# Two more rounding steps in each direction when the hidden activations are quantized

## The chip, the cores and the metric

The kernel runs on all eight cores of one Trainium2 chip. Each core computes one of eight batch rows with the same program and its own input, and the cores exchange nothing. The metric is the device time in microseconds of the slowest core. Each core has a TensorE (matrix products, called PE in the profile), a VectorE (DVE), a ScalarE (ACT), a GpSimd (POOL) and a SyncE (SP); the last two mostly issue DMA transfers here.

## The reference

One transformer layer on x of 8 x 2048 x 1024: causal attention with 16 heads and rotary embedding, a residual with layer norm, then a gated feed-forward block in which activations and weights are quantized, and again a residual with layer norm.

```python
def _act_quant(x):
    scale = 127.0 / jnp.clip(jnp.max(jnp.abs(x), axis=-1, keepdims=True), 1e-05)
    xq = jnp.clip(jnp.round(x * scale), -128.0, 127.0) / scale
    return x + jax.lax.stop_gradient(xq - x)

def _bitlinear(x, w):
    return jnp.einsum('bsi,oi->bso', _act_quant(x), _weight_quant(w))

x = _layernorm(x + _L0_attn_ref(x, L0_attn_w_qkv, L0_attn_w_out), axis=-1)
gate = jax.nn.silu(_bitlinear(x, w_gate))      # 1024 -> 4096
up = _bitlinear(x, w_up)                       # 1024 -> 4096
y = _bitlinear(gate * up, w_down)              # 4096 -> 1024
x = _layernorm(x + y, axis=-1)
```

`_weight_quant` makes every weight -1, 0 or 1 times one scale. What matters here is `_act_quant` of `gate * up`: each of 2048 rows has 4096 values that are scaled to at most 127 and rounded to an integer.

## The kernel before, in words

The first part of the program, up to about 1600 us of the span, computes attention, the first layer norm, the quantized input of the feed-forward block and the three weight matrices of -1, 0 and 1, which it leaves in device memory. The change does not touch it.

The second part is the feed-forward block. The 2048 rows are cut into four super-tiles (`j` from 0 to 3) of four row tiles (`k` from 0 to 3) with 128 rows each. For a super-tile TensorE runs the gate and up matmuls (lines 1653 and 1667), 32 groups of 128 x 512. ScalarE applies silu (line 1451), VectorE multiplies the two (line 1394) and keeps the largest absolute value of each row (lines 1400 to 1408). The product stays in SBUF as `h_h`, 4096 values a row.

Then the row tile is quantized by VectorE in `qchunks`, in four chunks of 1024 columns. A chunk is six instructions: scale and shift by 512 into `h_z` (line 1301), convert to int16 in `h_i` (1305), two compares that find out how the conversion rounded (1307 and 1310, into `h_u2` and `h_u3`), an add of the two results (1313), and the sum with an offset into `h_hq` (1316). TensorE turns `h_hq` by transposes into the PSUM tiles `p6t` (line 1688), and VectorE copies them to `h_hqT` (line 1373, written by `evacs`), eight copies a row tile.

The down projection (line 1627) of a super-tile is run by TensorE after the gate and up matmuls of the next super-tile, in two halves of 512 columns with 16 steps each. GpSimd loads its weights `h_td` (line 1581) into two buffers, one step at a time, each as soon as TensorE has emptied a buffer. At the end of a half VectorE copies four PSUM tiles to `h_os` with a scale (line 1329, written by `osbatch`). The second layer norm follows (`chainA`, `chainB`).

VectorE's order is written out by hand, and an engine runs its instructions in that order. For a super-tile after the first it is:

```python
qchunks(j, 0)
if j >= 1:
    osbatch(j - 1, 0)
qchunks(j, 1)
evacs(j, 0, 8)
qchunks(j, 2)
evacs(j, 8, 16)
qchunks(j, 3)
if j >= 1:
    osbatch(j - 1, 1)
evacs(j, 16, 24)
```

The other two `chainA` calls, the last copies and `chainB` come behind it, and then the scales and products of the next super-tile. Every instruction of `qchunks` has a drain before it, so that the one before has written its result. On TensorE the order is: gate and up of `j`, down of `j - 1`, the transposes of `j`, gate and up of `j + 1`.

Of the kernel before, what the change touches and what calls it, by code (L numbers as in the profile page):

```python
# [12 lines left out]
ALU = mybir.AluOpType  # L13
# [53 lines left out]
def build_program(stop_phase=99, debug=(), max_pairs=None, dbg_mode=None):  # L67
# [32 lines left out]
    with es:  # L100
# [5 lines left out]
        def CC(v):  # L106
            return s_consts[:, CIDX[v]:CIDX[v] + 1]
# [55 lines left out]
        def mk(stack, name, shape, dt=F32, side=None):  # L163
            kw = {} if side is None else {"side": side}
            return stack.enter_context(nc.sbuf_tensor(name, shape, dt, **kw))
# [1029 lines left out]
        s_z2 = mk(scH, "h_z2", [128, 1024])  # L1195
        s_i2 = mk(scH, "h_i2", [128, 1024], I16)
        s_u2 = mk(scH, "h_u2", [128, 1024], BF16)
        s_u3 = mk(scH, "h_u3", [128, 1024], BF16)
# [26 lines left out]
        def sc2c(j, k, w):  # L1225
            i = (j % 2) * NTS * 5 + k * 5 + SC2W[w]
            return s_sc2[:, i:i + 1]

        def hqb(j, k):
            return s_hq[(j * NTS + k) % 2]  # L1230
# [35 lines left out]
        def V(key, fn, waits=(), drain=False):  # L1266
            ve_ops.append((key, fn, waits, drain))
# [24 lines left out]
        def qchunks(j, k):  # L1292
            gt = j * NTS + k
            for c in range(4):
                cols = slice(c * 1024, (c + 1) * 1024)
                w = []
                if c == 0 and gt >= 2:
                    pj, pk = divmod(gt - 2, NTS)
                    w.append(("te", ("tr", pj, pk, 7)))
                V(("z2", j, k, c), lambda v, j=j, k=k, c=c, cols=cols:  # L1300
                    v.tensor_scalar(s_z2[:], s_h[k][:, cols],
                                    sc2c(j, k, "zq"), CC(512.0),
                                    ALU.mult, ALU.add),
                    waits=w, drain=True)
                V(None, lambda v: v.tensor_copy(s_i2[:], s_z2[:]),
                    drain=True)
                V(None, lambda v: v.scalar_tensor_tensor(  # L1307
                    s_u2[:], s_z2[:], -0.5, s_i2[:], ALU.add, ALU.is_ge),
                    drain=True)
                V(None, lambda v: v.scalar_tensor_tensor(  # L1310
                    s_u3[:], s_z2[:], 0.5, s_i2[:], ALU.add, ALU.is_ge),
                    drain=True)
                V(None, lambda v: v.tensor_tensor(
                    s_u2[:], s_u2[:], s_u3[:], ALU.add), drain=True)
                V(("hq", j, k, c), lambda v, j=j, k=k, c=c, cols=cols:
                    v.scalar_tensor_tensor(hqb(j, k)[:, cols], s_i2[:],
                                           -513.0, s_u2[:], ALU.add,
                                           ALU.add), drain=True)

        def osbatch(jd, h2):  # L1320
# [56 lines left out]
        for j in range(NSUP):  # L1377
# [14 lines left out]
            for gi in range(32):  # L1392
# [18 lines left out]
                if o == NCH - 1:  # L1411
                    qhead(j, k)
# [9 lines that stand above are left out]
# [19 lines left out]
        for j in range(NSUP):  # L1441
            for gi in range(32):
# [6 lines left out]
                elif j >= 1:  # L1449
# [4 lines left out]
                    drain=(gi <= 1))  # L1454
# [319 lines left out]
```

How the kernel before makes its waits and increments, by code:

```python
        @block.sync  # L202
        def _(sy):
            sy.wait_ge(dS.h, ph0_sync)
            for c in range(4):
                if c >= 1:
                    sy.wait_ge(tbv.h, c * 26)
                dS.dinc(sy.dma_start(out=s_gm[:],
                                     in_=d_t128[:, c * 512:(c + 1) * 512]))
                dS_tch[c] = dS.n
# [4 lines left out]
        @block.vector  # L215
        def _(v):
            for c in range(4):
                sl = slice(c * 512, (c + 1) * 512)
                v.wait_ge(dS.h, dS_tch[c])
                v.drain()
                tbv.inc(v.tensor_scalar(s_ga[:], s_gm[:],
                                        s_ifr[:, 0:1], CC(0.0),
# [36 lines left out]
                                            CC(0.0), ALU.mult, ALU.add))  # L259
                    v.drain()
                    tbv.inc(v.tensor_tensor(s_gs[:], s_gs[:], s_gm[:],
                                            ALU.subtract))
                    v.drain()
                    tbv.inc(v.tensor_scalar(s_gs[:], s_gs[:], CC(PI_CL),
                                            CC(NPI_CL), ALU.min, ALU.max))
                    v.drain()
                    if br == 0:
                        tb_sin[c] = tbv.n
                        v.wait_ge(tbs.h, 2 * c + 1)
                        v.drain()
                        tbv.inc(v.tensor_scalar(s_sin[:, sl], s_sin[:, sl],
                                                s_ifr[:, 2:3], CC(0.0),
# [1447 lines left out]
    @block.sync  # L1720
# [1 line left out]
        for c in ctrs:  # L1722
            if c.n:
                sy.wait_ge(c.h, c.n)
```

## Time and profile before

| | us |
|---|---|
| median of the timed runs (3) | 2928.35 |
| lowest and highest run | 2926.47, 2933.09 |
| profiled execution, device time | 2930.23 |
| its span on the slowest core (core 6) | 2928.6 |
| spans of the eight cores | 2906.9 to 2928.6 |
| VectorE busy, share of the span | 1355.8, 46% |
| TensorE busy, share of the span | 1604.0, 55% |

The profile is of one execution, on the slowest core unless another is named. Engine times are microseconds from the start of the span. A row of a group gives the line of the kernel, the engine, the operation, what is written from what, the shape, the count, the busy time and the mean of one, then the idle time before and what ended it. In an order of time, the first number is the start and the second the duration; in brackets stands the idle time before and what ended it.

### The profile page before, as it was taken

How to read it: one execution, taken by the hardware profiler on the slowest of the kernel's cores; microseconds unless marked ns; L12 is line 12 of the kernel's file. 1: busy time of each engine (PE TensorE's matmuls, PEld its weight loads, DVE VectorE, ACT ScalarE, POOL GpSimd, SP SyncE). 2: the span in 40 equal slices, each digit the busy share in tenths (PEclk: the TensorE clock that was granted, in tenths of full speed). 3: DMA queues.
4: the chain of work that ended last, by engine and by line, in shares of the span. 5: the costliest groups of instructions: out<-in, count | busy, mean ns of one | idle time of the engine just before them, and what ended most of it. 6: DMA issues, size and time to landing. Idle time of an engine off the chain costs nothing.

```text
span 2928.6 us, 23780 instructions; the slowest of 8 cores (2906.9 to 2928.6 us)
## 1 busy us (share of the span) xinstructions
PE 1604.0 (55%) x6348; PEld 649.7 (22%) x6348; DVE 1355.8 (46%) x2151; ACT 751.8 (26%) x1186; POOL 430.0 (15%) x684
## 2 busy tenths in 40 slices
PE   0597059999996731111110590496529762796263
PEld 0243013323332210000000240242214321342121
DVE  4404433343344343333343148745584649455733
ACT  0230036665664034443444120020012100210010
POOL 1000211111111123333334000001100020002021
PEclk9799558888887565555555795799859995899687
DMA  9000223333332179999999632044213420332032
GB/s 155 11 1 15 72 72 99 100 96 98 100 111 76 34 153 198 207 201 203 210 239 232 168 116 72 29 144 129 65 47 122 141 94 22 115 101 83 25 115 101
DMA packets 166725, 320.12 MB, mean 109 GB/s; under 512 B 30003, under 2 KB 99894, under 8 KB 166582
## 3 DMA queue, kind: packets, MB, share of 16 engines
q0 software_dynamic: 71168, 216.31, 31.1%
q1 hardware_dynamic: 95430, 102.29, 11.3%
q8 instruction: 58, 0.95, 0.1%
q14 instruction: 69, 0.57, 0.1%
HBM read 249.08 MB, written 71.30 MB: 109 GB/s over the span
## 4 chain that ended last, share of the span: by engine, by line
PE 42%; DMA 25%; DVE 16%; issue 7%; ACT 6%; DVEq 3%; POOL 2%; ACTq 0%; SPq 0%; POOLq 0%
DMA h_td<-ternd 7%; PE p6a L1653 7%; PE p6a L1667 7%; PE p_sc L537 6%; PE p_av L554 6%; PE p6a L1627 5%; DMA t_wst<-wuT 5%; DMA t_wst<-wgT 5%; PE p_qk L316 4%; DMA t_wst<-wdT 3%; PE p_sc L544 3%; ACT a_E L565 2%; PE p_qk L330 2%; PE p_R L797 2%; DVE h_u L1307 2%
## 5 line engine op out<-in xcount | busy, mean ns | idle before, releaser
L565 ACT ACTIVATE a_E<-p_sc 128x512 bf16<-128x512 f32 x640 | 333.5, 627 | 190.3 <-PE p_sc L544 102.7
L1627 PE MATMUL p6a<-h_td,h_hqT 128*128 128x512 bf16 x1024 | 268.7, 413 | 154.0 <-DMA h_td<-ternd 142.5
L537 PE MATMUL p_sc<-a_q,a_k 64*128 64x512 bf16 x640 | 241.9, 418 | 148.9 <-DMA e_sel<-sel 119.3
L1653 PE MATMUL p6a<-h_tg,h_xql 128*128 128x512 bf16 x1024 | 250.4, 389 | 88.8 <-DMA h_tu<-ternu 47.2
L999 PE MATMUL p_tr<-c_ident,f_xqtm 128*128 128x128 bf16 x128 | 16.2, 307 | 442.4 <-DVE f_xqtm L1090 442.4
L1667 PE MATMUL p6a<-h_tu,h_xql 128*128 128x512 bf16 x1024 | 244.5, 382 | 0.0
L1581 POOL DMA_DIRECT2D h_td<-ternd x128 | 92.0, 719 | 956.9 <-PE p6a L1627 935.2
L1451 ACT ACTIVATE h_sg<-p6a,h_sc 128x512 bf16<-128x512 f32 x128 | 88.0, 687 | 460.8 <-PE p6a L1653 316.0
L1688 PE MATMUL p6t<-c_ident,h_hq 128*128 128x128 bf16 x512 | 51.6, 280 | 281.2 <-DVE h_hqT L1373 250.1
L578 DVE TENSOR_REDUCE t_msum<-t_wst 128x1 f32<-128x1024 f32 x96 | 116.1, 1219 | 189.7 <-DMA t_wst<-wdT 69.3
L1394 DVE TENSOR_TENSOR h_h<-h_sg,p6a 128x512 f32<-128x512 bf16 x128 | 87.8, 686 | 247.9 <-PE p6a L1667 242.4
L554 PE MATMUL p_av<-a_E,a_v 128*65 128x512 bf16 x640 | 183.2, 439 | 2.9 <-ACT a_E L565 2.9
L1115 ACT ACTIVATE t_ta<-t_wst,p_thr 128x1024 bf16<-128x1024 f32 x96 | 109.9, 1145 | 276.7 <-DMA t_wst<-wuT 108.3
L316 PE MATMUL p_qk<-a_xfm,a_wqk 128*128 128x512 bf16 x512 | 116.1, 391 | 106.2 <-DMA a_wv<-wqkv 74.7
L1457 ACT ACTIVATE h_sg<-h_os 128x512 bf16<-128x512 f32 x16 | 10.1, 630 | 632.6 <-DVE h_os L1338 632.6
L1627 PEld LDWEIGHTS p6a<-h_td,h_hqT 128*128 128x128 bf16 x1024 | 99.8, 104 | 321.8 <-issue 243.4
L1653 PEld LDWEIGHTS p6a<-h_tg,h_xql 128*128 128x128 bf16 x1024 | 101.6, 100 | 214.3 <-issue 98.5
L1667 PEld LDWEIGHTS p6a<-h_tu,h_xql 128*128 128x128 bf16 x1024 | 101.2, 99 | 124.3 <-issue 6.2
L537 PEld LDWEIGHTS p_sc<-a_q,a_k 64*128 64x128 bf16 x640 | 56.9, 95 | 321.1 <-issue 309.7
L1044 DVE TENSOR_SCALAR f_st<-f_st,c_consts 128x1 f32<-128x1 f32 x16 | 4.4, 273 | 266.4 <-ACT f_tr L1126 266.4
L544 PE MATMUL p_sc<-a_masks,c_ident 128*128 128x512 bf16 x256 | 119.7, 468 | 0.0
L999 PEld LDWEIGHTS p_tr<-c_ident,f_xqtm 128*128 128x128 bf16 x128 | 12.4, 138 | 449.4 <-issue 449.4
(155 smaller groups left out, 2246.4 us busy)
## 6 DMA issues: line engine op xcount, KB each, us to landing
t_wst<-wgT POOLq DMA_DIRECT2D x64, 512.0 KB, 7.0
t_wst<-wuT POOLq DMA_DIRECT2D x64, 512.0 KB, 6.1
t_wst<-wdT POOLq DMA_DIRECT2D x64, 512.0 KB, 5.9
h_td<-ternd POOLq DMA_DIRECT2D x128, 256.0 KB, 3.2
h_tg<-terng SPq DMA_DIRECT2D x32, 1024.0 KB, 7.6
h_tu<-ternu SPq DMA_DIRECT2D x32, 1024.0 KB, 10.0
f_xt<-x SPq DMA_DIRECT2D x16, 512.0 KB, 9.3
y1s<-f_y1n SPq DMA_DIRECT2D x16, 512.0 KB, 6.3
```

The source lines that it names most:

```text
L316: mm = t.matmul(pb[:], s_wqk[:, kc * 2048 + sl * 128: kc * 2048 + (sl + 1) * 128], s_xfm[:, kc * S + ntile * 512: kc * S + (ntile + 1) * 512],
L537: mm = t.matmul(pb[:], s_k[hp * 64: hp * 64 + 64, ch * S + kc * 128: ch * S + (kc + 1) * 128], s_q[hp * 64: hp * 64 + 64, ch * S + j * 512 ...
L544: mm = t.matmul(pb[:], s_ident[:], s_masks[:, r * 512:(r + 1) * 512], start=False, stop=True)
L554: mm = t.matmul(pv[:], s_v[:, vbase: vbase + 65], s_E[:, kc * 512:(kc + 1) * 512], start=(kc == 0), stop=(kc == nkc[(h, j)] - 1))
L565: se.inc(s.activation(s_E[:, kc * 512:(kc + 1) * 512], p_sc[kc % 4][:], AF.Exp, bias=-CSTAB, scale=0.125))
L578: tpA.inc(v.tensor_reduce(s_msum[:, i6:i6 + 1], s_wst[i6 % 3][:], AXX, ALU.add, apply_absolute_value=True))
L1115: ts2.inc(s.activation(s_ta[i6 % 4][:], s_wst[(NWCH + i6) % 3][:], AF.Sign, bias=s_thr[:, 4 + mi6:5 + mi6], scale=1.0))
L1451: SEO(("silu", j, gi), lambda s, j=j, gi=gi, k=k: s.activation(s_sg[gi % 2][:], p_a[0 if gi % 2 == 0 else 2][:], AF.Silu, scale=sc2c(j, k, ...
L1581: dTd[dn % 2].dinc(g.dma_start(out=outap, in_=inap))
L1627: mm = t.matmul(p_a[k][:], s_hqT[k][:, kc * 128:(kc + 1) * 128], s_td[dn % 2][:, kk * 512:(kk + 1) * 512], start=(g2 == 0 and kk == 0), st ...
L1653: mm = t.matmul(pg[:], s_xql[j % 2][:, kc * 512 + k * 128:kc * 512 + (k + 1) * 128], s_tg[gs % 2][:, kc * 512:(kc + 1) * 512], start=(kc = ...
L1667: mm = t.matmul(pu[:], s_xql[j % 2][:, kc * 512 + k * 128:kc * 512 + (k + 1) * 128], s_tu[gs % 2][:, kc * 512:(kc + 1) * 512], start=(kc = ...
```

## The change

Where `qchunks` compared with two offsets (-0.5 and 0.5) and added the two results, it now compares with four (-0.5, -1.5, 0.5 and 1.5) and adds each to the running sum. The constant that is added at the end goes from -513 to -514, so that the quantized value is the same wherever the two further compares give 1 and 0.

```diff
                 V(None, lambda v: v.scalar_tensor_tensor(
                     s_u2[:], s_z2[:], -0.5, s_i2[:], ALU.add, ALU.is_ge),
                     drain=True)
-                V(None, lambda v: v.scalar_tensor_tensor(
-                    s_u3[:], s_z2[:], 0.5, s_i2[:], ALU.add, ALU.is_ge),
-                    drain=True)
-                V(None, lambda v: v.tensor_tensor(
-                    s_u2[:], s_u2[:], s_u3[:], ALU.add), drain=True)
+                for off in (-1.5, 0.5, 1.5):
+                    V(None, lambda v, off=off: v.scalar_tensor_tensor(
+                        s_u3[:], s_z2[:], off, s_i2[:], ALU.add, ALU.is_ge),
+                        drain=True)
+                    V(None, lambda v: v.tensor_tensor(
+                        s_u2[:], s_u2[:], s_u3[:], ALU.add), drain=True)
                 V(("hq", j, k, c), lambda v, j=j, k=k, c=c, cols=cols:
                     v.scalar_tensor_tensor(hqb(j, k)[:, cols], s_i2[:],
-                                           -513.0, s_u2[:], ALU.add,
+                                           -514.0, s_u2[:], ALU.add,
                                            ALU.add), drain=True)
```

Behind the compares, the lines of the changed kernel are one higher than before. The order of VectorE at the end of row tile 0 of super-tile 1, before: the last chunk, and then the first of the four copies behind the first half of the down projection, which waits for TensorE (`te`).

```order
L1301 TENSOR_SCALAR h_z2<-h_h0,h_sc2,c_consts 128x1024
L1305 CAST h_i2<-h_z2 128x1024
L1307 SCALAR_TENSOR_TENSOR h_u2<-h_z2,h_i2 128x1024
L1310 SCALAR_TENSOR_TENSOR h_u3<-h_z2,h_i2 128x1024
L1313 TENSOR_TENSOR h_u2<-h_u2,h_u3 128x1024
L1316 SCALAR_TENSOR_TENSOR h_hq0<-h_i2,h_u2 128x1024
L1329 TENSOR_SCALAR h_os0<-p6a0,h_sc2,c_consts 128x512 [waits te]
L1329 TENSOR_SCALAR h_os1<-p6a1,h_sc2,c_consts 128x512
```

After:

```order
L1301 TENSOR_SCALAR h_z2<-h_h0,h_sc2,c_consts 128x1024
L1305 CAST h_i2<-h_z2 128x1024
L1307 SCALAR_TENSOR_TENSOR h_u2<-h_z2,h_i2 128x1024
L1311 SCALAR_TENSOR_TENSOR h_u3<-h_z2,h_i2 128x1024
L1314 TENSOR_TENSOR h_u2<-h_u2,h_u3 128x1024
L1311 SCALAR_TENSOR_TENSOR h_u3<-h_z2,h_i2 128x1024
L1314 TENSOR_TENSOR h_u2<-h_u2,h_u3 128x1024
L1311 SCALAR_TENSOR_TENSOR h_u3<-h_z2,h_i2 128x1024
L1314 TENSOR_TENSOR h_u2<-h_u2,h_u3 128x1024
L1317 SCALAR_TENSOR_TENSOR h_hq0<-h_i2,h_u2 128x1024
L1330 TENSOR_SCALAR h_os0<-p6a0,h_sc2,c_consts 128x512 [waits te]
L1330 TENSOR_SCALAR h_os1<-p6a1,h_sc2,c_consts 128x512
```

The chunk has ten instructions in the place of six, and what stands behind it is the same. The order of VectorE between row tiles 2 and 3 of super-tile 1, before: row tile 2's last chunk, the eight copies of row tile 1's transposes, and the first instruction of row tile 3.

```order
L1301 TENSOR_SCALAR h_z<-h_h,h_sc,c_consts 128x1024
L1305 CAST h_i<-h_z 128x1024
L1307 SCALAR_TENSOR_TENSOR h_u<-h_z,h_i 128x1024
L1310 SCALAR_TENSOR_TENSOR h_u<-h_z,h_i 128x1024
L1313 TENSOR_TENSOR h_u<-h_u 128x1024
L1316 SCALAR_TENSOR_TENSOR h_hq<-h_i,h_u 128x1024
L1373 COPY h_hqT<-p6t 128x512 [waits te] x8
L1301 TENSOR_SCALAR h_z<-h_h,h_sc,c_consts 128x1024 [waits te]
```

After:

```order
L1301 TENSOR_SCALAR h_z<-h_h,h_sc,c_consts 128x1024
L1305 CAST h_i<-h_z 128x1024
L1307 SCALAR_TENSOR_TENSOR h_u<-h_z,h_i 128x1024
L1311 SCALAR_TENSOR_TENSOR h_u<-h_z,h_i 128x1024
L1314 TENSOR_TENSOR h_u<-h_u 128x1024
L1311 SCALAR_TENSOR_TENSOR h_u<-h_z,h_i 128x1024
L1314 TENSOR_TENSOR h_u<-h_u 128x1024
L1311 SCALAR_TENSOR_TENSOR h_u<-h_z,h_i 128x1024
L1314 TENSOR_TENSOR h_u<-h_u 128x1024
L1317 SCALAR_TENSOR_TENSOR h_hq<-h_i,h_u 128x1024
L1374 COPY h_hqT<-p6t 128x512 [waits te] x8
L1301 TENSOR_SCALAR h_z<-h_h,h_sc,c_consts 128x1024 [waits te]
```

Here too the four further instructions stand ahead of the copies, in each of the four chunks of row tile 2. No instruction of another engine has moved.

## Rows read from the trace of the kernel before

**Rows 1.** The page: the span, and busy time of each engine.

```profile
span 2928.6 us, 23780 instructions; the slowest of 8 cores (2906.9 to 2928.6 us)
...
PE 1604.0 (55%) x6348; PEld 649.7 (22%) x6348; DVE 1355.8 (46%) x2151; ACT 751.8 (26%) x1186; POOL 430.0 (15%) x684
```

**Rows 2.** Stretches: us, busy of PE, PEld, DVE, ACT, POOL (count), granted clock, DMA share, GB/s.

```profile
1758.00:1877.00 119.00, 13.69 (x130) 12.33 (x128) 108.43 (x142) 0.00 (x0) 0.00 (x0) 0.54 0.15 44
...
2101.00:2202.00 101.00, 21.80 (x162) 14.75 (x160) 84.68 (x148) 9.83 (x23) 2.49 (x4) 0.60 0.10 37
...
2412.00:2512.00 100.00, 21.07 (x156) 14.22 (x153) 84.67 (x148) 9.57 (x23) 2.48 (x4) 0.60 0.10 38
...
2720.00:2793.00 73.00, 12.46 (x125) 10.84 (x123) 67.63 (x92) 2.89 (x8) 2.49 (x4) 0.59 0.06 22
```

**Rows 3.** Waits of TensorE after 1600 us: total, times, longest.

```profile
PE p6t L1688 <- DVE h_hqT L1373: 250.1, 12, 27.9
...
PE p6t L1688 <- DVE h_hq L1316: 31.1, 1, 31.1
```

**Rows 4.** Groups of VectorE after 1600 us, the compare and the add.

```profile
L1310 DVE SCALAR_TENSOR_TENSOR h_u<-h_z,h_i 128x1024 bf16<-128x1024 f32 x64 | 78.4, 1225 | 5.9
...
L1313 DVE TENSOR_TENSOR h_u<-h_u 128x1024 bf16<-128x1024 bf16 x64 | 44.3, 692 | 5.9
```

**Rows 5.** VectorE in order of time, two chunks of super-tile 0.

```profile
1763.74 0.81 DVE L1301 TENSOR_SCALAR h_z<-h_h,h_sc,c_consts 128x1024 f32<-128x1024 f32 x1
...
1770.17 0.81 DVE L1301 TENSOR_SCALAR h_z<-h_h,h_sc,c_consts 128x1024 f32<-128x1024 f32 x1
```

**Rows 6.** VectorE in order of time, super-tiles 1 to 3: the long waits.

```profile
2046.20 2.97 DVE L1329 TENSOR_SCALAR h_os<-p6a,h_sc,c_consts 128x512 f32<-128x512 f32 x4 [27.38 <-PE p6a L1627]
...
2101.80 2.74 DVE L1373 COPY h_hqT<-p6t 128x512 bf16<-128x512 bf16 x8 [26.92 <-PE p6t L1688]
...
2361.97 2.96 DVE L1329 TENSOR_SCALAR h_os<-p6a,h_sc,c_consts 128x512 f32<-128x512 f32 x4 [23.19 <-PE p6a L1627]
...
2412.08 2.74 DVE L1373 COPY h_hqT<-p6t 128x512 bf16<-128x512 bf16 x8 [21.42 <-PE p6t L1688]
...
2670.42 2.97 DVE L1329 TENSOR_SCALAR h_os<-p6a,h_sc,c_consts 128x512 f32<-128x512 f32 x4 [20.88 <-PE p6a L1627]
...
2720.11 2.74 DVE L1373 COPY h_hqT<-p6t 128x512 bf16<-128x512 bf16 x8 [21.00 <-PE p6t L1688]
```

**Rows 7.** The same on core 0, super-tile 3.

```profile
2648.44 2.96 DVE L1329 TENSOR_SCALAR h_os<-p6a,h_sc,c_consts 128x512 f32<-128x512 f32 x4 [15.83 <-PE p6a L1627]
...
2696.75 2.74 DVE L1373 COPY h_hqT<-p6t 128x512 bf16<-128x512 bf16 x8 [19.59 <-PE p6t L1688]
```

**Rows 8.** TensorE in order of time after pauses, and once it runs.

```profile
1645.24 3.57 PE L1653 MATMUL p6a<-h_tg,h_xql 128*128 128x512 bf16 x8 [47.24 <-DMA h_tu<-ternu]
...
2130.73 3.57 PE L1688 MATMUL p6t<-c_ident,h_hq 128*128 128x128 bf16 x32 [25.66 <-DVE h_hqT L1373]
...
2202.16 3.57 PE L1653 MATMUL p6a<-h_tg,h_xql 128*128 128x512 bf16 x8 [20.94 <-ACT h_sg L1451]
...
2207.87 1.89 PE L1653 MATMUL p6a<-h_tg,h_xql 128*128 128x512 bf16 x8
```

**Rows 9.** Loads at line 1581: us, POOL busy (count), granted clock, DMA share, GB/s.

```profile
2364.90:2390.60 25.70, 5.70 (x8) 0.93 0.25 79
2673.40:2699.00 25.60, 5.74 (x8) 0.93 0.26 80
2390.60:2411.90 21.30, 4.26 (x6) 1.00 0.40 124
2699.00:2720.00 21.00, 4.26 (x6) 1.00 0.40 130
```

**Rows 10.** Groups of TensorE after 1600 us, the down projection.

```profile
L1627 PE MATMUL p6a<-h_td,h_hqT 128*128 128x512 bf16 x1024 | 268.7, 413 | 154.0 <-DMA h_td<-ternd 142.5 <-DVE h_os L1329 5.0 <-DVE h_h L1394 4.0
```

## The prediction

> **What bounds the kernel now.** Start with the totals [rows 1]: TensorE is busy 55% of the span and VectorE 46%, so neither is full and an average decides nothing. The question is which engine ends last in the stretch that the edit touches. The edit lies in the quantization of the hidden activations, which only runs after about 1760 us of the span, so the second view is the busy time by stretch [rows 2]. The reader sees four stretches, one for each super-tile, in which VectorE is busy for 108.43 of 119, 84.68 of 101, 84.67 of 100 and 67.63 of 73 us, while TensorE does 12 to 22 us of work. There VectorE sets the pace, and TensorE waits for it.
>
> The third view, TensorE's waits by tile, says the same from the other side [rows 3]: 250.1 us in 12 waits for the copies of the transposed activations (`h_hqT`), and 31.1 us in one wait for the first quantized tile. These are waits for VectorE's queue, in which the quantization of the next tile stands ahead of the copies.
>
> The fourth view is VectorE's own order of time. In super-tile 0, chunk follows chunk without a gap: one starts at 1763.74, the next at 1770.17 [rows 5], 6.43 us each. In super-tiles 1 to 3 VectorE does idle at two places, and there alone beside this work [rows 6]. After row tile 0 it waits for the first half of the down projection (27.38, 23.19 and 20.88 us), and after row tile 1 for the second half and the transposes behind it (26.92, 21.42 and 21.00 us). After row tiles 2 and 3 no such row exists.
>
> **The change, part by part.** It removes nothing. In each chunk it adds two compares of the kind of line 1310 and two adds of the kind of line 1313, with the same shapes, types and buffers, each behind a drain. The immediate values (-1.5, 1.5, and -514 for -513) change no shape. No DMA, wait or step of another engine is added or moved.
>
> Price of a chunk, from the groups by line [rows 4]: a compare takes 1225 ns, an add 692 ns. The gap before each is 5.9 us over 64, 0.092 us. So 2 x 1.225 + 2 x 0.692 + 4 x 0.092 = 4.20 us on top of 6.43. A row tile has 4 chunks: 16.81 us more (25.7 becomes 42.5). There are 16 row tiles: 268.9 us of VectorE work in all.
>
> Which of the 16 lie on the path:
> - Super-tile 0, four tiles: VectorE has no idle time, and the transposes and then the gate and up matmuls of super-tile 1 stand behind it. All four count: 67.2 us.
> - Super-tiles 1 to 3, row tile 0: the work grows into the wait for the down projection's first half. The waits of 20.88 to 27.38 us exceed 16.81, so 4 to 10.6 us are left and nothing shows. If that cover were gone, 16.8 us would show each time.
> - Row tile 1: the same with the second half, 21.00 to 26.92 us, so 4.2 to 10.1 us are left. Nothing shows.
> - Row tiles 2 and 3: VectorE runs without a wait from the first copies to the start of the next super-tile. Two tiles in three super-tiles: 6 x 16.81 = 100.9 us show.
>
> Sum: 10 x 16.81 = 168.1 us show and 6 x 16.81 = 100.9 us are hidden. What is late next after the hidden ones is still the down projection.
>
> The cover must hold on every core, since the slowest counts. The shortest wait of all cores is core 0's in super-tile 3, 15.83 us, with 19.59 us after it [rows 7]: there 1.0 us would show. I cost it at nothing.
>
> Two costs the trace of before shows only indirectly. First, TensorE's clock: the pauses that show grow from about 26 us (25.66 in one) to 42 us. In the four stretches the granted clock is already 0.54 to 0.60 [rows 2], near the lower of the two levels (1.2 of 2.4 GHz), and the first eight matmuls take 3.57 us after a pause of 20.94 us as after one of 47.24 us, against 1.89 us later on; the pause of 25.66 us ends in transposes [rows 8]. A longer pause costs what the short one does, and no new pause is made. I take 0; the ends are 0 and 13 x 1.7 = 22 us, if each of the 13 waits of [rows 3] paid once more what a restart costs (3.57 - 1.89).
>
> Second, GpSimd's loads of the down weights (`h_td`), which run beside the covered tiles. GpSimd issued 8 loads in 25.70 us and 8 in 25.60 us while VectorE quantized, and 6 in 21.30 and 6 in 21.00 us while it was idle [rows 9]: 3.2 us a load in the first case, 3.5 in the second. A busy VectorE does not slow them, so I take 0 here too.
>
> The Trainium skill ("SBUF — State Buffer", "Summary: rules for kernel authors") speaks against that: it says that descriptor generation for a DMA from GpSimd's queue starves while VectorE is in one of its faster modes. An add of 692 ns for as many elements as a compare of 1225 ns looks like such a mode. The same page, under "Who interferes with whom", says that an operation on two tensors has no mode that takes both ports, and the rows side with that. By the first rule the time would be that of the second rival below.
>
> The profiled execution took 2930.23 us (span 2928.6 us and 1.6 around it), 1.9 above the median of the timed runs, 2928.35. So 2930.2 + 168.1 = 3098.3 for a profile, and 3096.5 for the median: I forecast 3097 us, 5.7% slower.
>
> **The rivals.**
> 1. No cover: the six tiles beside the down projection show as well. For it: only 4 us of slack is left in super-tile 3 of the profiled core. Against it: the waits of rows 6 end with TensorE and not with VectorE, and they are longer than 16.81 us in all six cases there. It would give 2928.4 + 268.9 = 3197 us; one uncovered tile gives 16.8 us of that.
> 2. Starved loads: each load that falls into the 16.8 us of added work in a half of the down projection is held up by one added instruction, at most 1.225 us. With one load in 3.2 us that is 5 loads, 6.4 us in each of six halves: 39 us, so 3135 us. For it: TensorE waits 142.5 us for these loads already [rows 10], so a delay shows. Against it: rows 9.
> 3. Row tile 3's share hides behind the next super-tile's matmuls, which TensorE begins before VectorE is done. For it: two groups do run ahead. Against it: then TensorE stops for 20.94 us [rows 8], for the activation that needs VectorE's scales. In super-tiles 1 and 2 this would take back 2 x 16.8 us: 3063 us.
> 4. Not slower: the down projection's loads run ahead while VectorE holds the rest up, so that this stage goes at full rate. Its 1024 matmuls take 268.7 us and wait 142.5 us [rows 10]; at 1.89 us for eight they would take 242 us. That gives back 169 us against 168.1, and the time stays at 2928 us. It decides only if the whole of the waits goes and the clock stays up throughout. Against it: a load is issued only when TensorE has emptied one of two buffers, so it cannot run ahead during a pause, and a shorter half would uncover row tiles 0 and 1.
>
> That the change doesn't do what it says is excluded by the order of instructions, where VectorE has 64 x 4 more.
>
> **How the numbers follow.** Forecast 86%, rival 1 (in whole or for two or more tiles) 4%, rival 2 5%, rival 3 3%, rival 4 2%. Within the forecast, the spread of the runs before (2926.47 to 2933.09 us), single uncovered tiles on one core and part of the 22 us for the clock move the time by -12 to +20 us: 3085 to 3117. Towards rival 2 and rival 3 I widen it to 3080 to 3122, which leaves out most of the rivals' 14%. What a measurement can tell from no change is about 0.2%, 6 us; only rival 4 comes near it: faster 0.01, same 0.01, slower 0.98.
>
> **What would show it.** VectorE's busy time should rise by 64 x 3.83 = 245 us, with 192 compares at line 1311 of 1225 ns and 192 adds at line 1314 of 692 ns (128 more of each). A chunk should take 10.63 us. The six waits after row tiles 0 and 1 should shrink to 4 to 11 us, and TensorE's waits for `h_hqT` should grow by about 151 us, nine times 16.8, since the first of super-tile 0 is counted as a wait for `h_hq` (31.1 to 47.9 us). The gate, up and down stretches should keep their length. I am wrong if a wait of rows 6 vanishes and TensorE then waits in the down projection for VectorE, if loads of `h_td` take longer than 3.2 us each beside the compares, or if the compares with another constant take another time.

## The result and the profile after

The changed kernel takes 3099.28 us (median of 8 runs, 3089.37 to 3105.26) against 2931.02 us for the kernel before (8 runs, 2924.19 to 2938.24). The ratio is 1.0571, with a 95% interval from 1.0553 to 1.059: 168.3 us slower by the medians, 162 to 173 us by the interval. The forecast was 3097 us and 168.1 us more; that the two differ by 0.2 us is luck, since the interval is 11 us wide. Some executions are in a slower state, in which the cores of a die show a lower granted clock; the ratios here and below leave them out and the medians of the experiments do not, so a ratio need not be the quotient of two medians.

The page of the profiled execution after, whose slowest core is now core 4:

```profile
span 3103.6 us, 24181 instructions; the slowest of 8 cores (3071.5 to 3103.6 us)
...
PE 1578.4 (51%) x6237; PEld 647.0 (21%) x6348; DVE 1601.7 (52%) x2407; ACT 751.5 (24%) x1186; POOL 429.0 (14%) x684
```

VectorE's busy time rose from 1355.8 [rows 1] to 1601.7 us, by 245.9, on 256 more instructions. The span grew by only 175 us of these 246 (the medians differ by 168). TensorE's share fell from 55% to 51%, since the same program of TensorE stands in a longer span.

The stretches in which VectorE sets the pace, cut at the same events as in [rows 2], with the same columns:

```profile
1765.80:1952.30 186.50, 13.60 (x129) 12.21 (x128) 169.68 (x205) 0.00 (x0) 0.00 (x0) 0.52 0.10 28
2174.30:2309.50 135.20, 20.96 (x160) 15.20 (x159) 115.56 (x180) 9.84 (x23) 2.49 (x4) 0.56 0.07 27
2520.90:2654.20 133.30, 19.74 (x155) 14.00 (x153) 115.36 (x180) 9.58 (x23) 2.48 (x4) 0.56 0.08 28
2862.30:2969.20 106.90, 12.37 (x124) 10.80 (x122) 98.26 (x124) 2.89 (x8) 2.48 (x4) 0.55 0.05 15
```

They last 186.5, 135.2, 133.3 and 106.9 us in the place of 119, 101, 100 and 73: 67.5, 34.2, 33.3 and 33.9 us more, 168.9 together. That is the loss of the medians; the other 6 us of the 175 lie outside and are no more than executions of one kernel differ by. VectorE's busy time in the four grew by 61.3, 30.9, 30.7 and 30.6 us, and the gaps before the added instructions make up most of the rest, while TensorE's stayed at 12 to 21 us.

TensorE's waits by tile after 1600 us:

```profile
PE p6t L1689 <- DVE h_hqT L1374: 401.8, 12, 44.7
...
PE p6t L1689 <- DVE h_hq L1317: 47.9, 1, 47.9
...
PE p6a L1628 <- DVE h_os L1330: 6.8, 12, 1.5
```

The wait for the copies grew from 250.1 [rows 3] to 401.8 us, by 151.7 in the same 12 waits, and the one for the first quantized tile from 31.1 to 47.9 us.

The compares and adds of VectorE, by line:

```profile
L1311 DVE SCALAR_TENSOR_TENSOR h_u<-h_z,h_i 128x1024 bf16<-128x1024 f32 x192 | 235.2, 1225 | 17.7
L1314 DVE TENSOR_TENSOR h_u<-h_u 128x1024 bf16<-128x1024 bf16 x192 | 132.9, 692 | 17.7
```

There are 192 of each in the place of 64 [rows 4], at the same 1225 and 692 ns, with 17.7 us of gaps over 192, 0.092 us each. That is two compares and two adds more in each of 64 chunks; the two compares are one in each direction, and not two in each as the title can be read.

Two chunks of super-tile 0 in VectorE's order of time (start, then duration):

```profile
1771.51 0.81 DVE L1301 TENSOR_SCALAR h_z<-h_h,h_sc,c_consts 128x1024 f32<-128x1024 f32 x1
...
1782.15 0.81 DVE L1301 TENSOR_SCALAR h_z<-h_h,h_sc,c_consts 128x1024 f32<-128x1024 f32 x1
```

A chunk takes 10.64 us, where it took 6.43 [rows 5].

The six places after row tiles 0 and 1 of super-tiles 1 to 3, in VectorE's order of time (core 4):

```profile
2122.56 2.96 DVE L1330 TENSOR_SCALAR h_os<-p6a,h_sc,c_consts 128x512 f32<-128x512 f32 x4 [11.63 <-PE p6a L1628]
...
2175.13 2.94 DVE L1374 COPY h_hqT<-p6t 128x512 bf16<-128x512 bf16 x8 [7.09 <-PE p6t L1689]
...
2470.39 2.96 DVE L1330 TENSOR_SCALAR h_os<-p6a,h_sc,c_consts 128x512 f32<-128x512 f32 x4 [8.15 <-PE p6a L1628]
...
2521.01 2.74 DVE L1374 COPY h_hqT<-p6t 128x512 bf16<-128x512 bf16 x8 [5.07 <-PE p6t L1689]
...
2807.33 2.96 DVE L1330 TENSOR_SCALAR h_os<-p6a,h_sc,c_consts 128x512 f32<-128x512 f32 x4
...
2862.39 2.74 DVE L1374 COPY h_hqT<-p6t 128x512 bf16<-128x512 bf16 x8 [9.51 <-PE p6t L1689]
```

The waits that were 21 to 27 us [rows 6] are 11.63, 7.09, 8.15, 5.07, none and 9.51 us. At the fifth, in super-tile 3, the cover is used up. That was not this core alone: on cores 3 to 7 no wait of 1 us is left there, on cores 0 to 2 it is 1.9 to 4.9 us. In the kernel before this place was the tightest, with 15.83 us on core 0 [rows 7] and 16.4 to 20.9 us on the other seven, and the 20.88 us of the profiled core 6 [rows 6] was the longest of the eight. It cost little: TensorE's waits for the copies of line 1330 are 6.8 us in all on core 4, and 5.0 to 8.6 us over the eight cores, where they were 4.3 to 8.1 us before.

### The profile page after: what moved, and what is told of

Same layout as the page of the kernel before. It is cut to its first block, busy times and chain, and to the rows that moved or that the text cites. A ratio compares the mean times of both kernels' runs of the same rounds, so it can differ in the third digit from the quotient of the medians.

```text
span 3103.6 us, 24181 instructions; the slowest of 8 cores (3071.5 to 3103.6 us)
## 1 busy us (share of the span) xinstructions
PE 1578.4 (51%) x6237; PEld 647.0 (21%) x6348; DVE 1601.7 (52%) x2407; ACT 751.5 (24%) x1186; POOL 429.0 (14%) x684
## 4 chain that ended last, share of the span: by engine, by line
PE 37%; DMA 23%; DVE 21%; issue 7%; ACT 6%; DVEq 3%; POOL 2%; ACTq 0%; SPq 0%; POOLq 0%
PE p6a L1654 6%; PE p6a L1668 6%; DMA h_td<-ternd 6%; PE p_av L554 5%; DVE h_u L1311 5%; DMA t_wst<-wuT 5%; PE p_sc L537 5%; DMA t_wst<-wgT 5%; PE p6a L1628 4%; DMA t_wst<-wdT 4%; PE p_qk L316 3%; DVE h_u L1314 3%; ACT a_E L565 3%; PE p_sc L544 3%; PE p_qk L330 2%
## 5 line engine op out<-in xcount | busy, mean ns | idle before, releaser
L1628 PE MATMUL p6a<-h_td,h_hqT 128*128 128x512 bf16 x1003 | 263.0, 407 | 160.0 <-DMA h_td<-ternd 144.9
L1689 PE MATMUL p6t<-c_ident,h_hq 128*128 128x128 bf16 x512 | 52.2, 283 | 449.8 <-DVE h_hqT L1374 401.8
L1311 DVE SCALAR_TENSOR_TENSOR h_u<-h_z,h_i 128x1024 bf16<-128x1024 f32 x192 | 235.2, 1225 | 17.7
L1314 DVE TENSOR_TENSOR h_u<-h_u 128x1024 bf16<-128x1024 bf16 x192 | 132.9, 692 | 17.7
L1689 PEld LDWEIGHTS p6t<-c_ident,h_hq 128*128 128x128 bf16 x512 | 46.6, 131 | 456.2 <-issue 453.6
```

Source lines behind the costliest of these rows:

```text
L1311: V(None, lambda v, off=off: v.scalar_tensor_tensor(s_u3[:], s_z2[:], off, s_i2[:], ALU.add, ALU.is_ge), drain=True)
L1314: V(None, lambda v: v.tensor_tensor(s_u2[:], s_u2[:], s_u3[:], ALU.add), drain=True)
L1628: mm = t.matmul(p_a[k][:], s_hqT[k][:, kc * 128:(kc + 1) * 128], s_td[dn % 2][:, kk * 512:(kk + 1) * 512], start=(g2 == 0 and kk == 0), st ...
L1689: mm = t.transpose(pb[:, kk * 128:(kk + 1) * 128], hqb(j, k)[:, kc * 128:(kc + 1) * 128], s_ident[:])
```

## The experiments

In these experiments "covered" means row tiles 0 and 1 of super-tiles 1 to 3, and "exposed" the other ten. The edits of the first four are shown against the changed kernel, those of the last two against the kernel before. All times are compared with the kernel before, run again beside them. In the second to the fourth the loop over `offs` and the constant `base` stand as in the first and are left out here.

### The change in the covered row tiles alone

```diff
+                offs = (-1.5, 0.5, 1.5) if j >= 1 and k < 2 else (0.5,)
+                base = -514.0 if j >= 1 and k < 2 else -513.0
-                for off in (-1.5, 0.5, 1.5):
+                for off in offs:
...
-                                           -514.0, s_u2[:], ALU.add,
+                                           base, s_u2[:], ALU.add,
```

> The four further instructions of a chunk stand only in row tiles 0 and 1 of super-tiles 1 to 3 (6 of 16 row tiles); the other ten are as in the kernel before. Theory A (the down projection covers these six): the time stays at that of before, 2931 us within 6. Rival U (every row tile costs the same share of the measured 168 us): +63 us, 2994. Rival N (nothing is covered): 6 x 16.8 = +101 us, 3032. Rival S (GpSimd's weight loads are held up beside the added work): up to +39 us, 2970, and a longer down projection in the trace. In the trace, by A, VectorE's two waits of each super-tile shrink from 21 to 27 us to 4 to 11 us.

Measured: 2921.76 us against 2925.69, ratio 1.0011 (0.998 to 1.0041): no difference, at most 12 us more by the upper end. Rivals U (1.022), N (1.035) and the full price of S (1.013) lie outside the interval. VectorE's waits at the six places, core 5:

```profile
2033.52 2.97 DVE L1332 TENSOR_SCALAR h_os<-p6a,h_sc,c_consts 128x512 f32<-128x512 f32 x4 [10.57 <-PE p6a L1630]
...
2082.94 2.74 DVE L1376 COPY h_hqT<-p6t 128x512 bf16<-128x512 bf16 x8 [3.89 <-PE p6t L1691]
...
2341.95 2.96 DVE L1332 TENSOR_SCALAR h_os<-p6a,h_sc,c_consts 128x512 f32<-128x512 f32 x4 [4.26 <-PE p6a L1630]
...
2395.75 2.74 DVE L1376 COPY h_hqT<-p6t 128x512 bf16<-128x512 bf16 x8 [8.30 <-PE p6t L1691]
...
2651.09 2.96 DVE L1332 TENSOR_SCALAR h_os<-p6a,h_sc,c_consts 128x512 f32<-128x512 f32 x4 [1.82 <-PE p6a L1630]
...
2700.11 2.74 DVE L1376 COPY h_hqT<-p6t 128x512 bf16<-128x512 bf16 x8 [3.53 <-PE p6t L1691]
```

They are down to 1.82 to 10.57 us. Their sum on this core is 32.4 us, where the same core had 135.2 in the kernel before, some 103 us more. So VectorE did 101 us more work, and its waits paid for all of it. On six other cores no wait of 1 us is left at the fifth place, and the time does not show that.

### The change in the exposed row tiles alone

```diff
+                offs = (0.5,) if j >= 1 and k < 2 else (-1.5, 0.5, 1.5)
+                base = -513.0 if j >= 1 and k < 2 else -514.0
```

> The other ten row tiles alone have the four further instructions: all four of super-tile 0, and row tiles 2 and 3 of super-tiles 1 to 3. Theory A: the whole of the change's price, 10 x 16.8 = +168 us, 3099. Rival U (same share each): +105 us, 3036. Rival S: 168 less what the covered six then cost, up to 39, so 3060. By A, VectorE's two long waits of super-tiles 1 to 3 keep their 21 to 27 us, and TensorE's waits for the transposed copies grow by 9 x 16.8 = 151 us.

Measured: 3086.86 us against 2925.69, ratio 1.0565 (1.0527 to 1.0604), 154 to 177 us more: the price of the whole change (1.0571). U's 105 us is outside, and so is S's 129. TensorE's waits:

```profile
PE p6t L1691 <- DVE h_hqT L1376: 401.1, 12, 44.7
...
PE p6t L1691 <- DVE h_hq L1319: 47.9, 1, 47.9
```

They grew by 151.0 and 16.8 us, as in the changed kernel. VectorE's waits of super-tiles 1 and 3 in this kernel:

```profile
2104.94 2.97 DVE L1332 TENSOR_SCALAR h_os<-p6a,h_sc,c_consts 128x512 f32<-128x512 f32 x4 [28.57 <-PE p6a L1630]
...
2154.82 2.74 DVE L1376 COPY h_hqT<-p6t 128x512 bf16<-128x512 bf16 x8 [21.20 <-PE p6t L1691]
...
2788.31 2.97 DVE L1332 TENSOR_SCALAR h_os<-p6a,h_sc,c_consts 128x512 f32<-128x512 f32 x4 [18.16 <-PE p6a L1630]
...
2839.19 2.74 DVE L1376 COPY h_hqT<-p6t 128x512 bf16<-128x512 bf16 x8 [22.19 <-PE p6t L1691]
```

They lie within what the eight cores showed at these places in the kernel before (26.6 to 30.2, 19.8 to 26.9, 15.8 to 20.9 and 19.6 to 24.5 us), and so do the two of super-tile 2 (20.11 and 24.27 us): they kept their length. So ten row tiles cost everything and six cost nothing that shows, as the sum had it.

### Twice the addition in the covered row tiles

```diff
+                offs = (-2.5, -1.5, 0.5, 1.5, 2.5) if j >= 1 and k < 2 else (0.5,)
+                base = -515.0 if j >= 1 and k < 2 else -513.0
```

> Row tiles 0 and 1 of super-tiles 1 to 3 get twice the addition: eight further instructions in a chunk (offsets -2.5, -1.5, 0.5, 1.5, 2.5 after the first), 33.6 us a row tile; the other ten are as before. Theory A: the cover ends where VectorE's wait ends, so what shows is 33.6 less each wait of the kernel before, 6.2 + 6.7 + 10.4 + 12.2 + 12.7 + 12.6 = 61 us on the profiled core: 2992 us, 2980 to 3005 over the cores. Rival U: +126 us, 3057. Rival N: +202 us, 3133. If VectorE's work beside the down projection were free altogether: 2931.

Measured: 2997.04 us against 2925.69, ratio 1.0244 (1.0201 to 1.0288), 59 to 84 us more; theory A said 61 from one core's waits. TensorE's order of time on core 4 shows where:

```profile
2053.04 6.53 PE L1630 MATMUL p6a<-h_td,h_hqT 128*128 128x512 bf16 x15 [9.01 <-DVE h_os L1332]
...
2114.87 3.57 PE L1691 MATMUL p6t<-c_ident,h_hq 128*128 128x128 bf16 x32 [8.64 <-DVE h_hqT L1376]
...
2385.53 5.30 PE L1630 MATMUL p6a<-h_td,h_hqT 128*128 128x512 bf16 x10 [13.74 <-DVE h_os L1332]
...
2447.35 3.49 PE L1691 MATMUL p6t<-c_ident,h_hq 128*128 128x128 bf16 x32 [9.04 <-DVE h_hqT L1376]
...
2719.38 6.17 PE L1630 MATMUL p6a<-h_td,h_hqT 128*128 128x512 bf16 x15 [17.15 <-DVE h_os L1332]
...
2781.25 3.57 PE L1691 MATMUL p6t<-c_ident,h_hq 128*128 128x128 bf16 x32 [13.30 <-DVE h_hqT L1376]
```

At each of the six places TensorE now waits for VectorE, for the copies after the first half (9.01, 13.74 and 17.15 us) and after the first transposes (8.64, 9.04 and 13.30 us). The sum is 70.9 us, close to the loss by the ratio (0.0244 x 2925.69 = 71.4, with the interval above). The cover is a stock: what the down projection leaves VectorE idle is free, and what goes beyond it shows in full, as far as this one amount can tell. 33.6 us less 70.9 / 6 = 11.8 makes a stock of 21.8 us a place on this core; in the kernel before the same core waited 22.7 us a place (136.1 in all).

### Another kind of work in the covered row tiles

```diff
+                n1 = (5 if c < 2 else 4) if j >= 1 and k < 2 else 0
+                for _n1 in range(n1):
+                    V(None, lambda v: v.tensor_scalar(
+                        s_z2[:], s_z2[:], CC(1.0), CC(0.0),
+                        ALU.mult, ALU.add), drain=True)
```

The compares, the add and the constant of these row tiles are those of the kernel before.

> Row tiles 0 and 1 of super-tiles 1 to 3 get work of about the same length of another kind: 18 operations on one float32 input a row tile (multiply by 1, add 0, in place, the form of line 1301, 812 ns and a gap of 0.092: 16.3 us a row tile) in the place of compares and adds on two inputs. Theory A: what kind of work VectorE does is no matter, it is covered: 2931 us within 6. Rival S in the form of the Trainium skill (SBUF — State Buffer, Who interferes with whom: an operation with one input in a faster mode takes both ports and keeps GpSimd from writing descriptors): each of 5 loads in the added time of a half is held up by up to 0.81 us, 24 us over six halves, 2955, and the issue of a weight load takes longer than 0.72 us.

Measured: 2919.6 us against 2925.69, ratio 0.9991 (0.9967 to 1.0015): no difference. The added operations of VectorE, core 1:

```profile
L1314 DVE TENSOR_SCALAR h_z<-h_z,c_consts 128x1024 f32<-128x1024 f32 x108 | 88.0, 815 | 10.4
```

GpSimd's issues of the down weights on the same core, all 128 of them:

```profile
L1589 POOL DMA_DIRECT2D h_td<-ternd x128 | 95.2, 744 | 955.2 <-PE p6a L1635 933.3 <-issue 21.9
```

And the same group in the kernel with compares and adds in the covered row tiles, core 5:

```profile
L1584 POOL DMA_DIRECT2D h_td<-ternd x128 | 92.2, 721 | 957.9 <-PE p6a L1630 928.3 <-issue 26.5 <-DVE h_u L1313 2.9
```

The issue takes 744 ns on average here and 721 there. Over the eight cores it is 744 to 754 ns in this kernel, against 719 to 729 with the compares and adds and 716 to 723 in the kernel before. These means mix issues beside different work. The table sorts the single issues of these two kernels and of the kernel before (all cores, 1950 to 2800 us of the span) by what VectorE ran during the issue; those beside both kinds of operation are left out.

| VectorE during the issue | mean on a core, us | longest, us |
|---|---|---|
| nothing | 0.71 to 0.72 | 0.72 |
| only operations on two inputs (compares, adds, the sum with an offset) | 0.71 to 0.72 | 0.73 |
| only operations on one input (scale, conversion, the added ones) | 0.74 to 0.80 | 1.11 |

So operations on one input do hold GpSimd up a little, and operations on two inputs not measurably, which is the way the Trainium skill has it ("SBUF — State Buffer", "Who interferes with whom"). It is little: the longest issue took 0.4 us more than one beside an idle VectorE, half the length of an added operation, and over all 128 issues it is some 25 ns each, 3 us in sum, spread beside loads that come every 3.2 us [rows 9]. S, as it was priced (24 us, a ratio of 1.008), is outside the interval.

### The compares without the adds

```diff
+                for off in (-1.5, 1.5):
+                    V(None, lambda v, off=off: v.scalar_tensor_tensor(
+                        s_u3[:], s_z2[:], off, s_i2[:], ALU.add, ALU.is_ge),
+                        drain=True)
```

> In all 16 row tiles the two further compares alone, without their adds (their results are overwritten by the compare that stood there before). Theory A with the price by group: 2 x (1.225 + 0.092) = 2.63 us a chunk, 10.5 us a row tile, ten of them on the path: +105 us, 3036, and so 63 us of the 168 for the adds. Rival: a price per instruction whatever its kind (half of 168): +84 us, 3015. VectorE's long waits of super-tiles 1 to 3 should shrink by 10.5 us each.

Measured: 3018.48 us against 2917.84, ratio 1.0345 (1.0294 to 1.0396), 86 to 116 us more. The 105 us by group is inside, and the 84 by count is just outside. The trace tells them apart better; TensorE's waits:

```profile
PE p6t L1692 <- DVE h_hqT L1377: 345.9, 12, 38.5
...
PE p6t L1692 <- DVE h_hq L1320: 41.6, 1, 41.6
```

Both grew by 10.6 us a wait, 95.8 over nine and 10.5 for the one. An equal price per instruction would have made it 8.4. VectorE's six long waits on core 4 are 73.2 us in sum, where the same core had 136.1 in the kernel before: 10.5 less each, as expected.

### Two instructions in the place of six

```diff
                     v.tensor_scalar(s_z2[:], s_h[k][:, cols],
-                                    sc2c(j, k, "zq"), CC(512.0),
+                                    sc2c(j, k, "zq"), CC(12582912.0),
                                     ALU.mult, ALU.add),
                     waits=w, drain=True)
...
-                    v.scalar_tensor_tensor(hqb(j, k)[:, cols], s_i2[:],
-                                           -513.0, s_u2[:], ALU.add,
-                                           ALU.add), drain=True)
+                    v.tensor_scalar(hqb(j, k)[:, cols], s_z2[:],
+                                    CC(1.0), CC(-12582912.0),
+                                    ALU.mult, ALU.add), drain=True)
```

The four instructions between these two (the conversion, two compares and the add) are taken out, and the constants are added to the table.

> The other direction: a chunk of two instructions in the place of six. The scale adds 12582912 (1.5 x 2^23) in float32 in the place of 512, so that the result is already rounded to an integer (halves to the even one, as the reference rounds), and one further scale takes the constant off again and writes bfloat16. No conversion, compare or add is left. Theory A: 2 x (0.812 + 0.092) = 1.81 us a chunk against 6.43, 18.5 us less a row tile, ten of them on the path: -185 us, 2746; the six covered ones give nothing, and VectorE's waits there grow from 21 to 27 us to 39 to 45 us. If TensorE's transposes become the bound between the copies (3.6 us for 32 at the low clock beside 7.2 us of VectorE's work), up to 10 x 3.6 us of it are lost: 2782. Rival U (all 16 row tiles count in full): -296 us, 2635. Rival: the gain is given back by the down projection's loads: 2931.

Measured: 2728.44 us against 2917.84, ratio 0.9339 (0.9305 to 0.9373), 183 to 203 us faster. This version takes 6.6% less time than the kernel before. The two operations of VectorE, core 0:

```profile
L1307 DVE TENSOR_SCALAR h_hq<-h_z,c_consts 128x1024 bf16<-128x1024 f32 x64 | 52.0, 812 | 6.2
L1302 DVE TENSOR_SCALAR h_z<-h_h,h_sc,c_consts 128x1024 f32<-128x1024 f32 x64 | 52.0, 812 | 6.2
```

812 ns each, as expected, 1.81 us a chunk. TensorE's waits:

```profile
PE p6a L1618 <- DMA h_td<-ternd: 140.5, 97, 6.5
PE p6t L1679 <- DVE h_hqT L1364: 84.1, 12, 9.8
...
PE p6t L1679 <- DVE h_hq L1307: 12.6, 1, 12.6
```

The waits behind the quantization fell by 166.0 [rows 3] and 18.5 us, 184.5 together, nine and one row tiles of 18.5. That is the 185 of theory A. The bound by the transposes did not come. The ratio gives 193 us, 8 more than this, and the interval reaches down to it. VectorE's order of time at the six places in this kernel:

```profile
1959.88 2.96 DVE L1320 TENSOR_SCALAR h_os<-p6a,h_sc,c_consts 128x512 f32<-128x512 f32 x4 [43.06 <-PE p6a L1618]
...
2012.04 2.79 DVE L1364 COPY h_hqT<-p6t 128x512 bf16<-128x512 bf16 x8 [41.93 <-PE p6t L1679]
...
2233.18 2.97 DVE L1320 TENSOR_SCALAR h_os<-p6a,h_sc,c_consts 128x512 f32<-128x512 f32 x4 [39.33 <-PE p6a L1618]
...
2282.29 2.74 DVE L1364 COPY h_hqT<-p6t 128x512 bf16<-128x512 bf16 x8 [38.87 <-PE p6t L1679]
...
2499.05 2.97 DVE L1320 TENSOR_SCALAR h_os<-p6a,h_sc,c_consts 128x512 f32<-128x512 f32 x4 [35.10 <-PE p6a L1618]
...
2550.95 2.74 DVE L1364 COPY h_hqT<-p6t 128x512 bf16<-128x512 bf16 x8 [41.66 <-PE p6t L1679]
```

The waits are 35 to 43 us in the place of 21 to 27 [rows 6], 240.0 in sum, where the same core had 132.3 in the kernel before. So about 108 us of what VectorE saved in the six covered row tiles (6 x 18.5 = 111) went into waiting and brought nothing. TensorE's largest wait after 1560 us is now the one for the down weights, 140.5 us (142.5 in [rows 10]), which none of these kernels has touched.

## Why the prediction was right

- **Price of a chunk.** 4.20 us were forecast, 10.64 - 6.43 = 4.21 measured. It came from two groups of before with the same operation, shape and types, and from the gap before them. The experiment with compares alone shows that it is the sum of its parts: 10.6 us a row tile against 10.5 worked out.
- **Which row tiles count.** This was the step on which the forecast could have failed by 100 us: 10 of 16, chosen by whether VectorE's order of time has a wait behind the row tile. The two parts of the change, run apart, gave 1.0011 and 1.0565, and the whole 1.0571.
- **The depth of the cover.** 4 to 11 us were to be left at the six places. On core 4 it was 5 to 12 at five of them and none at the fifth. The detail was wrong and had no price. The 4 us came from the profiled core, whose wait at the fifth place was the longest of the eight. The prediction named core 0's 15.83 us as the exception, but core 2 had 16.41 us, also below 16.81, and five more cores had 17.5 to 20.3. A vanished wait was named as a sign of being wrong if TensorE then waits for VectorE in the down projection: the wait vanished, TensorE's did not follow (6.8 us against 5.0). Twice the addition showed how the price begins: not at once, but from the end of the wait.
- **What stands behind the copies.** TensorE's waits were to grow by 151 us and the first one to 47.9; it was 151.7 and 47.9.
- **TensorE's clock.** A longer pause was put at nothing, with up to 22 us as the other end. Two restarts of TensorE after:

```profile
2221.43 3.57 PE L1689 MATMUL p6t<-c_ident,h_hq 128*128 128x128 bf16 x32 [42.83 <-DVE h_hqT L1374]
...
2309.65 3.29 PE L1654 MATMUL p6a<-h_tg,h_xql 128*128 128x512 bf16 x8 [21.79 <-ACT h_sg L1452]
```

After 42.83 us the 32 transposes take 3.57 us, as after 25.66 us before [rows 8], and the first eight gate matmuls after 21.79 us take 3.29, not more than the 3.57 before. The granted clock of the four stretches was 0.54 to 0.60 [rows 2] and is 0.52 to 0.56: more of each is pause, and in a pause (2227 to 2268 us) it is 0.50, the lower of the two levels. It had no price that shows: the stretches grew by 67.5, 34.2, 33.3 and 33.9 us, and the further work of VectorE that lies on the path in them is 67.2 us in the first and 33.6 us in each of the other three.

- **The loads of the down weights.** They were put at nothing from [rows 9]. The covered part of the change cost nothing that shows, and the mean issue of a load took 719 to 729 ns there against 716 to 723 before; beside the compares and adds themselves it took 0.71 to 0.72 us, as beside an idle VectorE. The reading of [rows 9] was right for this change, though the loads there ran beside both kinds of operation.
- **The rivals.** No cover and starved loads, at their prices, are excluded by the covered row tiles alone (at most 12 us would be hidden in the interval), and the hiding of row tile 3 by the exposed row tiles alone and by the length of the stretches of super-tiles 1 and 2 (34.2 and 33.3 us more, where it would have been 16.8). The down projection's loads did not run ahead: TensorE's wait for them stayed at 144.9 us against 142.5 [rows 10].

## What to carry to other kernels

Before an edit is priced by its engine's total, look at each place where it stands for the wait behind it on the same engine: work that grows into a wait is free up to the wait's length and then costs in full, and where no wait follows, it costs in full at once. Read that wait on all cores and not on the profiled one alone: at one place here it was 15.8 to 20.9 us, and the profiled core had the longest. The same count says what an opposite edit brings: six instructions became two, and only the row tiles without a wait behind them paid it back.

## What the runs showed of the hardware

With 108 further VectorE operations on one float32 input (815 ns each) beside the loads, GpSimd's issue of a load took 744 to 754 ns on average on the eight cores; with further compares and adds on two inputs it took 719 to 729 ns, and in the kernel before 716 to 723 ns. Sorted by what ran during each issue, operations on two inputs alone left it at 0.71 to 0.72 us, as an idle VectorE did, and operations on one input alone made it 0.74 to 0.80 us on average and 1.11 us at most. That such operations hold the issue up was priced at up to 24 us; it was some 25 ns an issue, and the time did not show it.
